# A four-block transformer kernel on one core: first rotary stacks written in place, block attention projected once and fetched as DRAM row blocks

## What is computed

```python
x = x + rotary_attention(layernorm(x))  # affine norm, 16 heads of 64, rotary on all but the first row, full softmax
x = x + experts(layernorm(x))           # 8 experts 128 -> 512 -> 128, gelu, top 1, times its probability
x = x + block_attention(layernorm(x))   # 16 heads of 8; with scores = q k / sqrt(8):
#   allowed = (i // 32) >= (j // 32);  scores = where(allowed, scores, 0);  softmax over all j
#   q, k, v, out each with a bias
x = x + channel_mix(layernorm(x))       # mixes each row with the row before; sigmoid gate, squared relu
```

## Time and profile before

| | |
|---|---|
| median of 3 runs | 1501.4 us (1499.13 to 1502.56) |
| the profiled execution | 1499.58 us; span from the first to the last instruction 1497.8 us |
| mean granted TensorE clock | 0.925 of full speed |
| busy | TensorE 1301.8 us (87%), VectorE 819.5 (55%), ScalarE 888.6 (59%), GpSimd 291.6 (19%) |
| rotary attention: ahead of the loop, loop | 0 to 49.6, 49.6 to 912.8 us |
| experts | 912.8 to 1069 us |
| block attention: normalization, projection and first loads, main part | 1069 to 1081.4, 1081.4 to 1141.5, 1141.5 to 1463.6 us |
| channel mix | 1463.6 to 1497.8 us |

### The profile page before, as it was taken

One profiled execution on the slowest core, in us unless ns is written; L12 is line 12 of the kernel. 1 busy time (PEld: TensorE's weight loads), 2 busy tenths in 40 slices (PEclk: granted clock), 3 DMA queues, 4 the chain that ended last, 5 costly groups with the idle time before them and its releaser, 6 DMA issues. The chain is left out here.

```text
span 1497.8 us, 25780 instructions
## 1 busy us (share of the span) xinstructions
PE 1301.8 (87%) x8997; PEld 920.7 (61%) x8998; DVE 819.5 (55%) x1414; ACT 888.6 (59%) x1584; POOL 291.6 (19%) x218
## 2 busy tenths in 40 slices
PE   3799999999999999999999996197196999999985
PEld 2577677777777777777777774065064545454443
DVE  6355445555555554564554563254477767676616
ACT  3577677777777777776777772032153456555563
POOL 3123113212311311321331130400431000000000
PEclk9799999999999999999999997599586789999997
DMA  5544245235334433533533442411103111111001
GB/s 158 134 112 115 64 101 121 60 90 121 86 77 109 114 77 92 120 74 76 120 91 73 118 114 92 135 44 44 54 1 71 44 44 44 44 44 44 16 1 34
DMA packets 58403, 118.71 MB, mean 79 GB/s; under 512 B 10674, under 2 KB 31668, under 8 KB 58164
## 3 DMA queue, kind: packets, MB, share of 16 engines
q1 hardware_dynamic: 56868, 113.37, 31.0%
q0 software_dynamic: 1424, 3.67, 0.8%
HBM read 18.64 MB, written 5.31 MB: 16 GB/s over the span
## 5 line engine op out<-in xcount | busy, mean ns | idle before, releaser
L524 DVE TENSOR_REDUCE a_negmax<-a_score 128x1 f32<-128x1024 f32 x257 | 314.2, 1223 | 402.4 <-PE a_score L357 402.4
L465 ACT ACTIVATE a_probs_T<-a_tr 128x512 f32<-128x512 f32 x514 | 279.7, 601 | 213.5 <-PE a_tr L363 210.0
L471 ACT ACTIVATE a_probs<-a_score,a_negmax 128x1024 f32<-128x1024 f32 x256 | 288.3, 1126 | 10.6 <-DVE a_negmax L524 10.5
L363 PE MATMUL a_tr<-ident,a_probs 128*128 128x128 f32 x2056 | 267.8, 273 | 0.4 <-ACT a_probs_T L465 0.4
L363 PEld LDWEIGHTS a_tr<-ident,a_probs 128*128 128x128 f32 x2056 | 238.0, 141 | 40.7 <-issue 10.2
L371 PE MATMUL a_out<-a_probs_T,a_v 128*64 128x256 f32 x2112 | 242.5, 382 | 0.5 <-issue 0.5
L1430 DVE TENSOR_REDUCE a_lowest<-a_score 128x1 f32<-128x512 f32 (+3 forms) x320 | 181.8, 631 | 83.1 <-PE a_score L1319 44.2
L1400 ACT ACTIVATE a_probs_T<-a_score_T 128x1024 f32<-128x1024 f32 (+1 forms) x192 | 146.4, 810 | 123.9 <-PE a_score_T L1295 87.9
L371 PEld LDWEIGHTS a_out<-a_probs_T,a_v 128*64 128x64 f32 x2112 | 146.1, 137 | 77.9 <-issue 10.7
L318 POOL TENSOR_TENSOR a_rden<-a_rden_col,a_ones 128x256 f32<-128x256 f32 x65 | 68.3, 1052 | 593.2 <-DVE a_rden_col L547 593.2
L1315 PE MATMUL a_score<-a_k_cur,a_q_still 61*128 61x512 f32 (+3 forms) x320 | 103.6, 435 | 8.5 <-DVE a_lowest L1430 6.8
(11 more groups left out here) (253 smaller groups left out, 1950.2 us busy)
## 6 DMA issues: line engine op xcount, KB each, us to landing
a_xn_cur<-normed_T SPq DMA_DIRECT2D x17, 512.0 KB, 5.0
a_q_rot<-a_q_raw SPq DMA_DIRECT2D x68, 128.0 KB, 2.4
a_k_rot<-a_k_raw SPq DMA_DIRECT2D x68, 128.0 KB, 2.3
a_k_stack0ah<-a_k_hi SPq DMA_DIRECT2D x18, 256.0 KB, 3.3
a_k_stack0al<-a_k_lo SPq DMA_DIRECT2D x18, 256.0 KB, 5.0
a_k_stack0bh<-a_k_hi SPq DMA_DIRECT2D x18, 256.0 KB, 5.0
a_k_stack0bl<-a_k_lo SPq DMA_DIRECT2D x18, 256.0 KB, 4.8
a_k_stack1ah<-a_k_hi SPq DMA_DIRECT2D x16, 256.0 KB, 3.3
```

The lines of the kernel that those rows point to most:

```text
L363: last = nc.tensor.transpose(tr_ps[k // 4][:, k % 4 * P:k % 4 * P + P], probs[s % 4][:, k * P:k * P + P], core.ident[:])
L465: nc.scalar.activation(probs_T[(s - 1) // 4 % 2][:, h, 4 * i:4 * i + 4, tile % 2 * P:tile % 2 * P + P], tr_ps[i][:].rearrange("p (k q) -> ...
L471: nc.scalar.activation(probs[s % 4][:], score_ps[s % 2][:], ACT.Exp, bias=negmax[:, s:s + 1], accum_out=den[:, s:s + 1]).then_inc(probs_re ...
L524: nc.vector.tensor_reduce(negmax[:, s:s + 1], score_ps[s % 2][:], axis=AX.X, op=ALU.max, negate=True)\
```

## The change

In the first rotary pair, ScalarE writes the high parts straight into their 64 rows of the stacks, head by head, and VectorE writes the keys' low parts so; only the copies into the other 64 rows go by DMA, six in place of twelve, with one semaphore for each head. VectorE does the product of the keys that was GpSimd's. Two of the tiles that GpSimd zeroed are zeroed by ScalarE (a copy of the identity times 0), and one memset is issued once x is normalized. The loop starts on `first_stacked[1]`.

A class `BlockOperands` holds block attention's operand tiles and constants from the experts' stage on: the constants are loaded between the two small routing loads, ScalarE writes the mask's rows into 14 tiles after the routing's exponential, GpSimd writes the suffix counts ahead of the scatter.

In block attention the weights are transposed beside the normalization. Queries and keys are projected once, without repetition (8 steps, batch 0 first), into `q_hi`, `q_lo`, `k_hi`, `k_lo`. SyncE stores these into DRAM tensors, each part twice, in the order of an operand tile's 32 rows; an operand load is then a block of 32 rows in DRAM. Group 0's rows are stored and loaded in the projection block, those of groups 1 to 3 at the start of the main block, those of batch 1 in the turn of group 1. The value projection goes with steps 5 to 8, and the suffix sums come last. The output's bias becomes a product of one row on TensorE, added to each of the output projection's 16 products.

```diff
-                sp.wait_ge(hi_ready[0], 1)
-                stack_q(0, 0, 0, first_stacked)
-                sp.wait_ge(hi_ready[1], 1)
-                stack_k(0, 0, 0, first_stacked)
...
-                for part in range(2):
-                    stack_q(0, 1, part, stacked[0])
-                    stack_k(0, 1, part, stacked[1])
+                for h, key_hi, query_lo, key_lo in ((0, (first_hi, 2), (first_lo, 1), (first_lo, 2)), (1, (hi_ready[1], 1), (lo_ready[0], 1), (lo_ready[1], 1))):
+                    own, other = slice(64 * h, 64 * h + 64), slice(64 - 64 * h, 128 - 64 * h)
+                    sp.wait_ge(*key_hi)
+                    sp.dma_start(k_stack[0][h][0][other, :].bitcast(F32), k_stack[0][h][0][own, :].bitcast(F32)).then_inc(first_stacked[h], 16)
+                    sp.wait_ge(*query_lo)
+                    sp.dma_start(q_stack[0][h][other, :].bitcast(F32), lo[0][own, :].bitcast(F32)).then_inc(first_stacked[h], 16)
+                    sp.wait_ge(*key_lo)
+                    sp.dma_start(k_stack[0][h][1][other, :].bitcast(F32), k_stack[0][h][1][own, :].bitcast(F32)).then_inc(first_stacked[h], 16)
...
-                nc.gpsimd.memset(probs[3][:], 0.0)
-                nc.gpsimd.memset(probs_T[0][:], 0.0)
-                nc.gpsimd.memset(probs_T[1][:], 0.0)
-                nc.gpsimd.memset(v[1][:], 0.0)
...
-                nc.gpsimd.tensor_tensor(raw[1][:], raw[1][:], tables[:, 2, :], ALU.mult).then_inc(rotated[1], 1)
...
+                nc.gpsimd.memset(probs_T[0][:], 0.0).then_inc(zeroed, 1)
+                pool.wait_ge(xn_ready, 4)
+                nc.gpsimd.memset(probs_T[1][:], 0.0).then_inc(zeroed, 1)
...
+                act.wait_ge(ident_ready, 2)
+                for rows in (v[1][:], probs[3][:].rearrange("p (k q) -> p k q", k=TB)):
+                    blank = core.ident[:].rearrange("p (o q) -> p o q", o=1).broadcast_to([P, TB, P])
+                    nc.scalar.activation(rows, blank, ACT.Copy, scale=0.0).then_inc(rows_zeroed, 1)
...
-                    nc.scalar.activation(hi[i][:], raw[i][:], ACT.Copy).then_inc(hi_ready[i], 1)
+                    for h, done in ((0, first_hi), (1, hi_ready[i])):
+                        rows = slice(64 * h, 64 * h + 64)
+                        nc.scalar.activation((q_stack[0][h], k_stack[0][h][0])[i][rows, :], raw[i][rows, :], ACT.Copy).then_inc(done, 1)
...
                 sp.dma_start(switch[:], sw).then_inc(small_loaded, 16)
+                operands.load(sp)
...
+                operands.count(pool)
                 pool.wait_ge(places_ready, 1)
...
                 nc.scalar.activation(expd[:], shifted[:], ACT.Exp).then_inc(expd_ready, 1)
+                operands.fill(act)
...
+        def store_rows(sp, i, b, heads, stored):
+
+            rows, cols = slice(DH1 * heads.start, DH1 * heads.stop), slice(b * N, b * N + N)
+            for part in range(2):
+                for again in range(2):
+                    to = q_rows[heads, again, part, :, cols] if i == 0 else k_rows[heads, part, again, :, cols]
+                    sp.dma_start(to, parts[i][part][rows, cols].bitcast(F32)).then_inc(stored, 16)
+
+        def load_rows(sp, to, head_rows, m, landed):
+            for hp in range(2):
+                for x in range(2):
+                    rows = head_rows[m % G * HG + 2 * hp + x, :, :, :, m // G * N:m // G * N + N].rearrange("r p d n -> (r p d) n")
+                    sp.dma_start(to[hp][64 * x:64 * x + 32, :].bitcast(F32), rows).then_inc(landed, 16)
...
+                    sp.wait_ge(stack_ready, 2)
+                    store_rows(sp, 0, 0, slice(0, HG), q_stored[0])
+                    sp.wait_ge(stack_ready, 4)
+                    store_rows(sp, 1, 0, slice(0, HG), k_stored[0])
+                    sp.wait_ge(q_stored[0], 64)
+                    load_still(sp, 0)
+                    sp.wait_ge(k_stored[0], 64)
+                    load_keys(sp, 0)
+                    load_moving(sp, 0)
...
+                store_rows(sp, 0, 0, slice(HG, H1), q_stored[1])
+                store_rows(sp, 1, 0, slice(HG, H1), k_stored[1])
+                sp.wait_ge(q_stored[1], 64)
+                load_still(sp, 1)
+                sp.wait_ge(k_stored[1], 64)
+                load_keys(sp, 1)
...
-                        ins = nc.tensor.matmul(score_ps[n % 3][:, t * D:t * D + D], attn_T[:, t * P:t * P + P], wo_T[:], start=True, stop=True)
+                        nc.tensor.matmul(score_ps[n % 3][:, t * D:t * D + D], attn_T[:, t * P:t * P + P], wo_T[:], start=True, stop=False)
+                        ins = nc.tensor.matmul(score_ps[n % 3][:, t * D:t * D + D], one_row[:], bo_row[:], start=False, stop=True)
```

More of the change, by code:

```diff
@@ L110, in _ @@
             def _(pe):
+                if pe_first is not None:
+                    pe_first(pe)
                 for t in range(T):
@@ L912, in _, with __init__, load, fill @@
                                                    op0=ALU.mult, op1=ALU.add)
-def block_attention(nc, core, consts, Wq, bq, Wk, bk, Wv, bv, Wo, bo):
+class BlockOperands:
+    def __init__(self, nc, stack, core, block):
+        sb = lambda n, s, dt=F32: stack.enter_context(nc.sbuf_tensor(f"a1_{n}", s, dt))
+        self.nc, self.block = nc, block
+        self.suffix = sb("suffix", [P, B, 2, H1, DH1 + 1])
+        self.q_still = [[sb(f"q_still{i}{hp}", [P, N], F32R) for hp in range(2)] for i in range(2)]
+        self.q_moving = [[sb(f"q_moving{i}{hp}", [P, N], F32R) for hp in range(2)] for i in range(2)]
+        self.k_cur = [[sb(f"k_cur{i}{hp}", [P, N], F32R) for hp in range(2)] for i in range(3)]
+        self.fixed = sb("fixed", [P, BLOCK_CONSTS])
+        self.fixed_loaded, self.suffix_cleared = core.sem("a1_fixed_loaded"), core.sem("a1_suffix_cleared")
+    def load(self, sp):
+        sp.dma_start(self.fixed[:], self.block).then_inc(self.fixed_loaded, 16)
+    def fill(self, act):
+        act.wait_ge(self.fixed_loaded, 16)
+        for tiles, i in ((self.q_still, 0), (self.q_moving, 0), (self.k_cur, 1)):
+            rows = self.fixed[:, 920 + P * i:920 + P * i + P].rearrange("p (t k) -> p t k", t=1).broadcast_to([P, TB, P])
+            for pair in tiles:
+                for tile in pair:
+                    self.nc.scalar.activation(tile[:].rearrange("p (t k) -> p t k", t=TB), rows, ACT.Copy)
+    def count(self, pool):
+        self.nc.gpsimd.memset(self.suffix[:], 0.0).then_inc(self.suffix_cleared, 1)
+        pool.wait_ge(self.suffix_cleared, 1)
+        pool.wait_ge(self.fixed_loaded, 16)
+        for i in range(2):
+            left = self.fixed[:, 768 + 4 * i:772 + 4 * i].rearrange("p (g h) -> p g h", g=1).broadcast_to([P, H1 // HG, HG])
+            for b in range(B):
+                self.nc.gpsimd.tensor_copy(self.suffix[:, b, i, :, DH1].rearrange("p (g h) -> p g h", g=H1 // HG), left)
+def block_attention(nc, core, operands, q_rows, k_rows, Wq, bq, Wk, bk, Wv, bv, Wo, bo):
     G = H1 // HG
@@ new lines, in _ @@
+                        if k >= 4:
+                            project_v(k - 4)
+                    pe.wait_ge(v_added, 4)
+                    pe.wait_ge(operands.fixed_loaded, 16)
+                    for bh in range(2 * B):
+                        b, half = bh // 2, bh % 2
+                        for kt in range(4 * half, TB):
+                            off = min(kt - 4 * half, 4)
+                            ins = nc.tensor.matmul(sums_ps[:, bh * P:bh * P + P], fixed[:, off * P:off * P + P], v_den[:, b, kt, :, 0:DH1],
+                                                   start=kt == 4 * half, stop=kt == TB - 1)
@@ L1074, in _ @@
                         dve.wait_ge(high_ready[k % 2], k // 2 + 1)
[L1075 to L1079 removed]
+                        nc.vector.tensor_tensor(parts[i][1][:, cols], full[k % DEPTH][:], parts[i][0][:, cols].bitcast(F32), ALU.subtract).then_inc(stack_ready, 1)
@@ L1624, in rope_tables @@
     return np.stack([cos * s, sin * s, cos, sin]).astype(np.float32)
-def part_signs():
-    low = np.tile(np.repeat(np.array([[0, 0, 1, 1], [0, 1, 0, 1]]), DH1, axis=1), (1, HG))
-    return np.stack([1 - 2 * low[0], low[0], 1 - 2 * low[1], low[1]], axis=1).astype(np.float32)
 def block_consts():
@@ L1675 @@
         a[name] = nc.dram_tensor(f"in_{name}", arrays[f"in_{name}"].shape, F32, kind="ExternalInput").ap()
-    for name, value in (("rope", rope_tables()), ("part", part_signs()), ("block", block_consts())):
+    for name, value in (("rope", rope_tables()), ("block", block_consts())):
         arrays[f"const_{name}"] = value
@@ L1681 @@
     slots = [nc.dram_tensor(f"slots_{n}", (blocks * P, D), F32, kind="Internal").ap() for n, blocks in (("x", SLOT_BLOCKS), ("y", SLOT_BLOCKS + 1))]
-    build(nc, a, c, slots, out)
+    head_rows = [nc.dram_tensor(f"rows_{n}", shape, F32, kind="Internal").ap() for n, shape in (("q", (H1, 2, 2, DH1, B * N)), ("k", (H1, 2, 2, DH1, B * N)))]
+    build(nc, a, c, slots, head_rows, out)
     return _run(nc, [arrays], core_ids=[0]).results[0]["out"]
```

286 lines of the change are left out of this document (109 added, 177 removed).

## The result

The changed kernel takes 1474.19 us (median of 4 runs, 1473.56 to 1474.61); the kernel before, on the same chip, 1500.64 (1499.13 to 1502.56). The ratio is 0.9823, 95% interval 0.9806 to 0.9840: 26 us faster, where 46 were forecast. The profiled execution took 1474.61, its span 1471.4, 26.4 less than the span before (1497.8).

The account below looks back on a forecast made before the run. Waits for stack transfers at the start and repeated projections ahead of block attention's first score were taken to bound the kernel; -11.9 + 1.0 - 36.8 + 1.5 = -46.2 us gave 1455 against the median, range 1447 to 1466.

Parts of the forecast that it names:

- The start: Rotary attention up to its loop: the loop starts at 37.7 us instead of 49.6, a gain of 11.9 us.
- the variance's release: Start of rotary attention: VectorE's variance no longer held up by GpSimd's memsets, ending near 6.6 us; gain 4.53 us.
- The rival that the variance stays long: At the start, ScalarE's copies or the 128x4096 memset end late and the 4.53 us stay: 1459.5 us, chance 8%.
- The experts' load: Routing: a small routing load follows the 588 KB of constants and delays the chain by 0.4 to 1.9 us, taken as +1.0.
- Block attention's first part: From block attention's normalization to its first score: repeated projections go, 23 us instead of 60; -36.8 us.
- VectorE's chain: Before block attention's first score: VectorE's operand work after the projections was to end last, giving the first score at 1104.7 us.
- SyncE's chain: Before block attention's first score: 20 issues of stores and loads plus waits, done at 1101 us, 3 us ahead of VectorE.
- the first rival: Block attention's first stores run on only four DMA engines; first score 9.6 us later, result 1464.6 us; chance 15%.
- the forecast's cover: Behind block attention's first score: further stores and eight loads land before the twentieth fill, hidden by 3 us or more.
- The output bias becomes 16 more products ... +1.5 (0 to 3): Block attention's output projections: about 1.0 us for the last four bias products on the tail, 0.5 for the rest.
- The clock rival: TensorE's clock goes otherwise in block attention: 1449 us if the main part starts warm, 1462 if projections stay slow; chance 16%.
- the prediction's own signs of being wrong: Quarter DMA share in first stores with the score waiting for keys; variance still long; first score to end changing over 6 us.

Follow-up runs that it names:

- undone in three ways: Changed kernel with the bias added by VectorE (1462.36 us), with bias products of 128 rows (1462.50 us), or with one product of one row by 512 columns (1460.95 us).

## Why the prediction was half right

**The start** was right term by term: the variance's release, the moved product, three transfers and then six at the rate of the old ones (33.8 and 37.6, against 33.9 and 37.7). The rival that the variance stays long did not come.

**The experts' load** was the right mechanism with too small a size: +2.9 where 1.0 was taken and 1.9 was the upper bound. The small load was issued 0.5 us later and landed 5.0 us after its issue, where it took 2.6 in the kernel before. The forecast's range had only the issue and the time of the 588 KB at one of two rates. In the trace they move near the faster one (362 GB/s between 918.6 and 919.9) and have landed at 920.6; the small load lands 1.9 us behind that, at 922.5, and next to nothing moves in between (4 GB/s between 920.2 and 921.2). With the bytes' 1.5 us at the faster rate on top of its old 2.6, it would have landed at 921.6: the last 0.9 us are what the range left out, and what they are stays open. The run with the load behind gives 2.4 to 2.6 of the delay back.

**Block attention's first part** was right in its sum, -37.0 for -36.8, by two errors that cancelled. VectorE's chain was done 20.8 us after the first projection, not 22.7, as the clock rose 3.5 us after the first projection's start and not behind the fourth step. SyncE's chain was sized at 19.6 and took 22.6, since the stores ran on four engines. That was the first rival's mechanism, and the rule cited from the Trainium skill (DMA: Bandwidth & Descriptors, "Why a DMA increments its semaphore by 16 and not by 1") is borne out: 0.26 of the engines busy with four heads outermost, 0.97 with 32 rows, and 0.74 with the twelve heads of the next stores. Its price was not 9.6: an engine among four moved 98 / 4 = 25 GB/s, the faster of the two rates that the rival weighed, with which it said "no loss".

**Behind the first score** the forecast's cover held: no wait for a load at the twentieth fill. The step that failed is "The output bias becomes 16 more products ... +1.5 (0 to 3)". Products of one row were priced by the row of products of 128 rows, and the twelve ahead of the tail were put at 0.5, as if hidden, where TensorE is busy for 9.7 of the 10 us behind the first four. They cost 11.3 us in the projections' own time (part of it in the last one, at the low clock), and some 4.4 more in the work around them, where the clock was low for longer: together 15.7 where 1.5 was forecast, so some 14 of the 20 us that were missing. The loop's 3.3 and the routing's 1.9 are nearly all of the rest. The same is shown in the kernel before (+15.7), and undone in three ways (-12.4 to -13.9).

The sentence "the rotary loop and main part of block attention keep their code, so only the stretches ahead of them ... can move" was wrong twice: the main part's projections did not keep their code, and unchanged code moves with the clock. The clock rival had the right suspect in the wrong place. Two of the prediction's own signs of being wrong came: a DMA share of a quarter during the first stores (0.26), and the 356 us from the first score to the end, which became 372.

**The loop's 3.3 us** stay open. In this one profile there are two spells at 1.2 GHz behind the loop's turn, where TensorE idles for 2.29 and 2.24 us; here the second:

```profile
785.00:789.10 4.10, 1.86 (x15) 1.53 (x14) 1.65 (x2) 3.06 (x4) 0.00 (x0) 1.00 0.03 4
789.10:792.70 3.60, 3.60 (x13) 3.10 (x14) 1.62 (x3) 1.11 (x3) 0.28 (x1) 0.53 0.02 5
```

Other profiles have none, one or two such spells. The second profile of the kernel before has none, and its loop takes 866.2 us against 863.5 in the first, so most of the 3.3 lies within what its own executions differ by.

## What to carry to other kernels

Price an added product by a row with its own number of rows, and look at what stands before and behind it: a bias of one row between products of 128 rows cost 2.2 us here where the products that it serves take 1.2, so give it 128 rows, or one product for the whole bank, or another engine. A small load that a chain waits for goes ahead of a large one on the same queue. When a DMA's outermost dimension is small, read the DMA share: a quarter means four engines of sixteen, and another order of the rows in DRAM brought in the others, at twice the rate.

## What the runs showed of the hardware

- At full speed (clock 1.00) products of two passes start 0.42 us apart where 128 rows and 1 row alternate, and 0.22 where all read 128 rows: 0.19 us for each change.
- TensorE's clock fell to 1.2 GHz at the end of such stretches or just behind, although the engine was busy without a gap as far as its modelled ends tell: 15 of 18 times, and 0 of 21 without them.
- Four DMA engines storing from 32 partitions moved 98 GB/s, sixteen 206: twice, not four times as much, so that one engine of four is nearly twice as fast as one of sixteen (25 against 13 GB/s).
- A load of 4 KB issued behind one of 588 KB on the same queue landed 5.0 us after its issue and 1.9 behind the large one; 2.6 us after its issue where no such load stood ahead of it.
